# Gate of experts 2 to 6 in seven block products: 21 matmuls of 256 columns for 12 of 512, and the sums they need

## The reference, cut to what matters

```python
h = _layernorm(x) * (1 + cb) + sb
gate = einsum('btd,edf->ebtf', h, Wg)     # + low rank h @ Ga @ Gb for two of the experts
up   = einsum('btd,edf->ebtf', h, Wu)     # + low rank
mid  = silu(gate) * up
out  = einsum('ebtf,efd->ebtd', mid, Wd)  # + low rank
x    = x + gb * einsum('bte,ebtd->btd', router_weights(h), out)
```

## Time and profile before

| what | value |
|---|---|
| median of 3 runs | 804.85 us (803.84 to 805.88) |
| the profiled execution's own time | 805.75 us |
| its span, first to last instruction | 804.0 us |
| PE busy | 793.1 us, 99% of the span |
| POOL busy | 403.3 us, 50% |
| DVE, ACT busy | 508.3 us, 465.8 us |
| mean granted TensorE clock | 0.998 of full speed |

### The profile page before, as it was taken

One profiled execution on the slowest core, in us unless ns is written; L12 is line 12 of the kernel. 1 busy time (PEld: TensorE's weight loads), 2 busy tenths in 40 slices (PEclk: granted clock), 3 DMA queues, 4 the chain that ended last, 5 costly groups with the idle time before them and its releaser, 6 DMA issues.

```text
span 804.0 us, 14773 instructions
## 1 busy us (share of the span) xinstructions
PE 793.1 (99%) x5116; PEld 710.0 (88%) x5116; DVE 508.3 (63%) x1074; ACT 465.8 (58%) x1259; POOL 403.3 (50%) x547
## 2 busy tenths in 40 slices
PE   9899999999999999999999999999999999999997
PEld 8688899999999999999999999898888888888887
DVE  5667676475466667457557757666785454554575
ACT  5777677677577767767667866652553232332322
POOL 3767587486567567567657656220311010110493
PEclk9999999999999999999999999999999999999999
DMA  9200010000000000000000000202410110100002
GB/s 334 104 28 1 2 61 1 1 8 2 0 8 2 1 4 5 1 2 8 1 1 8 1 1 2 79 1 53 118 40 2 40 40 1 40 0 1 1 1 106
DMA packets 8329, 22.32 MB, mean 28 GB/s; under 512 B 1592, under 2 KB 4280, under 8 KB 8128
## 3 DMA queue, kind: packets, MB, share of 16 engines
q1 hardware_dynamic: 7680, 21.29, 7.9%
q10 hardware_dynamic: 576, 0.08, 0.1%
HBM read 19.26 MB, written 2.11 MB: 27 GB/s over the span
## 4 chain that ended last, share of the span: by engine, by line
PE 94%; DVE 2%; ACT 1%; issue 1%; POOL 1%; DMA 1%; ACTq 0%; DVEq 0%; POOLq 0%
PE ps_o L671 14%; PE ps_proj L548 9%; PE ps_proj L550 9%; PE ps_proj L549 9%; PE ps_s L548 7%; PE ps_s L549 7%; PE ps_s L550 7%; PE ps_turn L600 4%; PE ps_y L548 4%; PE ps_y L549 4%; PE ps_y L550 4%; PE ps_turn L618 3%; PE ps_turn L548 2%; PE ps_turn L549 2%; PE ps_turn L550 2%; PE ps_o L550 2%
## 5 line engine op out<-in xcount | busy, mean ns | idle before, releaser
L671 PE MATMUL ps_o<-vaug,probs 128*128 128x129 f32 x1024 | 136.1, 276 | 1.7 <-POOL probs L1674 0.9
L671 PEld LDWEIGHTS ps_o<-vaug,probs 128*128 128x128 f32 x1024 | 130.0, 192 | 8.0 <-POOL probs L1674 1.4
L993 ACT ACTIVATE ps_s<-ps_s,knorm 128x512 f32<-128x512 f32 x128 | 79.3, 657 | 96.2 <-PE ps_s L550 96.1
L1287 DVE RECIPROCAL rden<-ps_o 128x2 f32<-128x2 f32 x128 | 21.8, 170 | 155.5 <-PE ps_o L671 155.3
L1680 POOL TENSOR_TENSOR we_lo<-raw_e,we_hi 128x512 fp32r<-128x512 f32 x22 | 28.4, 1318 | 161.3 <-ACT we_hi L1036 161.3
L1257 DVE TENSOR_TENSOR prod<-ps_proj,cs 128x1024 f32<-128x1024 f32 x76 | 92.5, 1218 | 11.0 <-ACT sq L936 11.0
L1625 POOL TENSOR_TENSOR root<-ssq,powers 128x4 f32<-128x4 f32 x76 | 77.8, 1024 | 27.4 <-ACT sq L936 27.4
L936 ACT ACTIVATE sq<-ps_proj 128x128 f32<-128x128 f32 x304 | 80.1, 279 | 18.9 <-PE ps_proj L550 16.0
L1641 POOL TENSOR_TENSOR prod<-prod 128x512 f32<-128x512 f32 x62 | 80.1, 1292 | 10.0 <-DVE prod L1257 10.0
L548 PE MATMUL ps_proj<-w_hi,h_hi 128*128 128x512 f32 x192 | 83.3, 434 | 0.4 <-DVE h_lo L1204 0.4
L1672 POOL TENSOR_SCALAR_AFFINE_SELECT probs<-probs 128x256 f32<-128x256 f32 x64 | 26.4, 412 | 106.7 <-ACT probs L1001 106.4
(11 more groups left out here) (220 smaller groups left out, 2191.2 us busy)
## 6 DMA issues: line engine op xcount, KB each, us to landing
raw_e<-in_we SPq DMA_DIRECT2D x8, 768.0 KB, 4.4
raw_p<-in_wqkv SPq DMA_DIRECT2D x6, 512.0 KB, 8.5
raw_e<-in_wo SPq DMA_DIRECT2D x4, 512.0 KB, 12.7
x_all<-in_x SPq DMA_DIRECT2D x1, 1536.0 KB, 7.3
out<-acc SPq DMA_DIRECT2D x3, 512.0 KB, 2.6
x_all<-in_wmod SPq DMA_DIRECT2D x1, 1024.0 KB, 10.4
gates_a<-gate_rows_dram SPq DMA_DIRECT2D x8, 128.0 KB, 2.9
gates_b<-gate_rows_dram SPq DMA_DIRECT2D x1, 1024.0 KB, 10.2
```

The lines of the kernel that those rows point to most:

```text
L671: mm = pe.matmul(ps_o[:, h * (D + 1):(h + 1) * (D + 1)], probs[:, s % 2, at:at + P], vaug[b % 2][:, k, i // 2, :], start=(h == 0 and k == ...
L993: act.activation(ps_s[:, t, :], ps_s[:, t, :], ACT.Tanh, scale=knorm[:, b % 2, t, i // 2:i // 2 + 1]).then_inc(tanh_done, 1)
```

## The change: what it does

**The product.** For the tiles of experts 2 to 6 (8 to 27, `SEVEN` to `EIGHT`) gate is a 2 x 2 block product of weights (256 x 256) and tokens (256 x 512), made in seven products of blocks in place of eight. Each is one `three` of 256 columns. Four of the seven (`seven_first`) go ahead of up, the other three (`seven_last`) between up and the products with Wd. ACT copies the four first results to `seven`, POOL makes three sums of them, DVE adds two to the late results.

**What the blocks need.** Sums of blocks of the tokens (`sums_t`, four POOL instructions of 128x256 for each n) and of the weights (`sums_s`, four of 128x128 for each expert), and the high and low parts of these (`round_t`, `rest_t`, `round_s`, `rest_s`). The tokens of batches 4 and 5 are written to DRAM and read back, since their place is taken by then.

**The places.** `low_rank` and `fold` pieces move a tile earlier, split_e(2, 0) and (2, 1) move ahead within tiles 6 and 7, router piece 5 moves from tile 7 to 6, and `part` has a buffer for each n.

```diff
-LATE_ROUTE = {2 * NEXT + 3: [0], 2 * NEXT + 4: [1, 2], 2 * NEXT + 5: [3, 4], 2 * NEXT + 6: [5, 6, 7], 2 * NEXT + 7: [8, 9, 10, 11, 12]}
+LATE_ROUTE = {2 * NEXT + 3: [0], 2 * NEXT + 4: [1, 2], 2 * NEXT + 5: [3, 4, 5], 2 * NEXT + 6: [6], 2 * NEXT + 7: [7, 8, 9, 10, 11, 12]}
-LOW_STEPS = {NEXT + 1: [0, 1], NEXT + 2: [2], NEXT + 4: [3], NEXT + 5: [4, 5]}
+LOW_STEPS = {NEXT + 1: [0], NEXT + 2: [1, 2], NEXT + 3: [3], NEXT + 4: [4, 5]}
@@ PE
+            def seven_first(m):
...
+                if m == FIRST_OF[e]:
+                    pe.wait_ge(we_split, 3 * e - 1)
+                    pe.wait_ge(s_split, e - NL + 1)
+                if m == FIRST_OF[NL] + n:
+                    pe.wait_ge(t_split, 2 * n + 2)
+                if q:
+                    pe.wait_ge(quarter_silu, 2 * q - 1)
+                else:
+                    pe.wait_ge(mid_done, 2 * SEVEN - 1)
+                product_of(ps_s[:, 0, 0:S], of["A11"], of["B11"], True)
+                product_of(ps_s[:, 0, S:], of["S2"], of["T2"], False).then_inc(seven_ready, 1)
+                if q:
+                    pe.wait_ge(quarters_added, q)
+                product_of(ps_s[:, 1, 0:S], of["S1"], of["T1"], True)
+                product_of(ps_s[:, 1, S:], of["S3"], of["T3"], False).then_inc(seven_ready, 1)
+            def seven_last(m):
...
+                pe.wait_ge(seven_copied, 2 * q + 1)
+                product_of(ps_s[:, 0, 0:S], of["A12"], of["B21"], False).then_inc(gu_ready, 1)
+                pe.wait_ge(seven_copied, 2 * q + 2)
+                product_of(ps_s[:, 1, 0:S], of["S4"], of["B22"], False)
+                product_of(ps_s[:, 1, S:], of["A22"], of["-T4"], False).then_inc(gu_ready, 1)
+            for m in range(SEVEN, EIGHT):
+                seven_first(m)
+                up_alone(m)
+                seven_last(m)
+                down(2 * m - 2)
+                down(2 * m - 1)
@@ ACT
+            def round_t(n):
+                act.wait_ge(t_made, 4 * n + 4)
...
+                elif n == 2:
+                    act.wait_ge(t_split, 4)
+                    act.wait_ge(router, 3 * STEPS)
...
+                if m == NEXT + 2:
+                    round_s(NL)
                 mid_head(2 * m + 1)
...
+                if m == NEXT + 3:
+                    split_e(NL, 2)
+                    round_t(2)
+            for m in range(SEVEN, EIGHT):
+                copy_seven(m)
+                for e, m3 in SEVEN_SPLIT.get(m, ()):
                     split_e(e, m3)
+                if m in SEVEN_ROUND:
+                    round_s(SEVEN_ROUND[m])
+                if m == SEVEN + 2:
+                    round_t(3)
+                silu_seven(m)
+                mid_head(2 * m)
+                mid_head(2 * m + 1)
@@ DVE
+            for m in range(SEVEN, EIGHT):
+                add_quarters(m)
+                for g in (2 * m, 2 * m + 1):
+                    product_seven(g)
+                for g in (2 * m, 2 * m + 1):
+                    mid_tail(g)
+                accumulate(2 * m - 2)
+                accumulate(2 * m - 1)
@@ POOL
+            inv_std2(B - 1)
+            low_rest(0)
+
+            pool.wait_ge(h2_split, B)
+            sums_t(2)
+            split_e(NL, 0)
+            sums_s(NL)
+            rest_s(NL)
+            low_rest(1)
+            rest_t(0)
+            split_e(NL, 1)
+            rest_t(1)
+            for m in range(SEVEN, EIGHT):
+                sums_seven(m)
+                if m == SEVEN:
+                    split_e(NL, 2)
+                    rest_t(2)
+                if m == SEVEN + 1:
+                    sums_t(3)
+                if m == SEVEN + 2:
+                    rest_t(3)
+                if m in SEVEN_SUMS:
+                    sums_s(SEVEN_SUMS[m])
+                for e, m3 in SEVEN_SPLIT.get(m, ()):
                     split_e(e, m3)
+                if m in SEVEN_ROUND:
+                    rest_s(SEVEN_ROUND[m])
```

More of the change, by code:

```diff
@@ L522, in _ @@
             sp.wait_ge(router, 2 * STEPS)
+            for kept in h2_kept:
+                sp.wait_ge(kept, 16)
             expert(1)
@@ L846, in _ @@
                 slot(s)
-            for m in range(NEXT, len(TILES)):
+            for m in range(NEXT, SEVEN):
                 up(2 * m)
@@ L858, in _ @@
                     low_rank(i)
+            for m in range(SEVEN, EIGHT):
[4 more added lines that the diff above has]
+                down(2 * m - 1)
+                for i in LOW_STEPS.get(m, ()):
+                    low_rank(i)
+            for m in range(EIGHT, len(TILES)):
+                up(2 * m)
+                up(2 * m + 1)
+                down(2 * m - 2)
+                down(2 * m - 1)
             down(2 * len(TILES) - 2)
@@ L1391, in accumulate @@
                     dve.wait_ge(base_done, 2 * n + half + 1)
[L1392 to L1394 removed]
+                if e == NE - 1 and n == 0 and half == 0:
+                    dve.wait_ge(low_ready, 3 * NL)
                 for t in range(2):
@@ L1585, in _ @@
                         route(LATE, piece)
+            for m in range(SEVEN, EIGHT):
[6 more added lines that the diff above has]
+                accumulate(2 * m - 1)
+                for i in LOW_STEPS.get(m, ()):
+                    fold(i)
+            for m in range(EIGHT, len(TILES)):
+                product(2 * m)
+                product(2 * m + 1)
+                mid_tail(2 * m)
+                mid_tail(2 * m + 1)
+                accumulate(2 * m - 2)
+                accumulate(2 * m - 1)
             accumulate(2 * len(TILES) - 2)
@@ L1727, in slot @@
                         split_e(e, m3)
+                if s in SLOT_SUMS:
+                    sums_t(SLOT_SUMS[s])
                 return units[1:]
@@ L1740, in _, with low_rest @@
                 pending = slot(s, pending)
-            inv_std2(B - 1)
-            for e in range(NL):
+            def low_rest(e):
                 pool.wait_ge(low_rounded, 2 * e + 2)
+                pool.wait_ge(ln2_rstd, B) if e == 0 else pool.wait_ge(s_split, 1)
                 pool.tensor_tensor(lowA_both[R:P, e], lowA[R:P, e], lowA_both[R:P, e], ALU.subtract).then_inc(low_split, 1)
```

204 lines of the change are left out of this document (186 added, 18 removed).

## The result

The changed kernel takes 808.88 us (median of 6 runs, 807.09 to 809.65) where the kernel before takes 804.84 (6 runs, 803.84 to 805.88): a ratio of 1.0044, 95% interval 1.0028 to 1.0059. By the medians it is 4.0 us slower, by the ratio 3.5 (1.0044 x 804.85 = 808.4); 810 was predicted. The profiled execution took 809.65 us, the slowest of the six, with a span of 807.9. It is compared with the span of 804.0 before: +3.9.

The account below looks back on a forecast made before the run. PE bounds the kernel (busy 99%, 94% of the chain). Tile 9's start +10.0, the other 19 tiles -5.1 and tile 11 +0.4 give +5.3 on 804.85: 810.1, said as 810; own range 806.5 to 813, 8 in 10 801 to 813.

Parts of the forecast that it names:

- tile 9's start: End of the entry through tile 8: tile 9 at 613.6 against 603.6, +10.0 us with tile 8's gain included.
- The gain in PE's work: Gate of tiles 8 to 27: 21 matmuls of 256 columns replace 12 of 512, saving 0.24 to 0.29 us a tile.
- Steady state: Later seven-product tiles: PE takes 8.1 us each, slack 1 us or more at each step, so additions cost nothing.
- The 0.4 us at tile 11 to 12: Tightest tile, 11: POOL's sums, two splits and rest_s take 8.5 us against PE's 8.1, costing 0.4 us.
- POOL's list and product(14): Entry to tile 8: POOL's preparations end at 600.0; DVE, held by POOL, finishes product(14) at 597.7 instead of 591.1.
- The first wait: Ahead of tile 8's first gate matmuls: PE 4.1 us late, waiting for DVE's product(14).
- accumulate(12): DVE behind router pieces 7 to 12, six steps held by POOL: done at 609.7 instead of 599.1.
- The second wait: Ahead of tile 8's products with Wd: PE waits some 6 us, released by an accumulate on DVE.
- The mechanism: Entry: a DVE instruction reading two SBUF operands waits for the running POOL instruction's end, one such per POOL instruction.
- Rival 1: Entry: DVE is hardly held up by POOL, only 1.4 us lost; 801.3 us, chance 0.18.
- Rival 2: Entry: product(14) and copy late, but pieces 7 to 12 mostly fall in POOL's gap; 804 us, chance 0.15.
- Rivals 3 and 4: Gate pace of 256 columns: 0.125 with late entry, 812.3 us; or 0.13, gain only 0.2 us; chance together 0.07.

Follow-up runs that it names:

- the two runs that fill that wait: Changed kernel with low-rank matmuls repeated to keep PE busy in both waits (807.41 us, ratio 1.0031) or only the second (807.49 us, 1.0028).
- the two runs in which product(14) came early enough: Changed kernel with router pieces 3 to 6 behind product 15's mid_lo (812.17 us), or with POOL's entry instructions cut to 256 columns (804.72 us).
- moved preparations and whole pieces: Changed kernel with its preparations, router Exp, round_s and first-results copy in other places, POOL's instructions uncut: 803.69 us, ratio 0.9978 to the kernel before.
- run with halves: Changed kernel with POOL's entry instructions cut into pieces of 256 columns, preparations not moved: 804.72 us, ratio 0.9997 to the kernel before.
- first try: Changed kernel with POOL's four t_lo subtractions of token groups 0 and 1 moved ahead of tile 5's end: 806.77 us, ratio 1.0012.
- second wait filled: Changed kernel with six repeats of a low-rank step on PE ahead of tile 8's Wd products only: 807.49 us, ratio 1.0028.
- POOL's row beside the kernel before: Kernel before, with ten more POOL subtractions of 128x512 behind its split of expert 2's first weights, results unread: 814.70 us, ratio 1.0112.
- pieces moved: Changed kernel with router pieces 3 to 6 put behind mid_lo of index 15, together with pieces 7 to 12: 812.17 us, ratio 1.0075.

## Why the prediction was right, step by step

- **Time and direction.** 810 was said, 808.88 measured; slower, as forecast. +5.3 us was the sum and +3.9 is the trace's. That tile 9's start fits to 0.4 us is owed in part to luck: two errors of the entry, 2.1 us too much and 1.6 too little, cancel (below).
- **The gain in PE's work.** 5.1 us over the last 19 tiles was too small: 5.7 measured. The pace of 256 columns was 0.118 where 0.1196 was taken. Tiles take 8.03 to 8.16 us where 8.1 was said.
- **Steady state.** No wait in any tile from 9 to 27. The 0.4 us at tile 11 to 12 did not come.
- **POOL's list and product(14).** Forecast: done at 597.7; the row says 596.93 + 0.69 = 597.6. POOL's list was to end at 600.0 and ended at 596.58 + 2.90 = 599.5. The first wait, forecast 4.1 us, was 3.4. The list began 0.7 us later than said, since PE was 0.4 us earlier and not 0.8 and ACT's first Copy was done at 582.5 and not 581.8, and it grew by 1.1 us and not by some 2. One sum of the prediction is off (588.6 + 3.0 is 591.6, not 591.4), and nothing hangs on it, since DVE's next step ends with POOL's instruction in any case.
- **accumulate(12).** This step was mis-sized. It was to be done at 609.7, behind six hindered steps; it was done at 607.6. In pieces 7 to 12 five steps were hindered (0.69, 0.44, 0.63, 0.96 and 1.00 us), since POOL was idle from 599.5 to 601.8 and its sums of 128x256 take 0.74 and not 0.83. The second wait was 3.0 us where 6 was said: accumulate(12) came 2.1 us earlier, and PE came to it at 604.8 and not at 603.3.
- **The missing term.** PE's clock after a wait stood in the sum at nothing. By the timeline it costs 1.6 us behind the second wait, by the traces of the two runs that fill that wait 1.4 us, by their ratios 1.0 to 1.3 us (1.0031 and 1.0028 for 1.0044, with intervals that overlap); the one behind the first is hidden by the second wait (the same two runs). By the trace together: 2.1 too much for accumulate(12), 1.6 too little for the clock. Tile 9 starts at 613.2 where 613.6 was said.
- **The mechanism.** That POOL's instructions hold DVE up is shown, not only argued: ten of them alone slow the kernel before by 9 us, and cutting them in half without taking any away gives back 3.8. Rival 1 (DVE hardly held, 801.3) is out; its time is what comes of the change once the row of POOL is moved and cut, 800.0. Rival 2 (half of it, 804) is out by the second wait. Rivals 3 and 4 are out by the pace of 0.118. What the prediction had as a wait for DVE alone, ahead of tile 8, has POOL's own list as a second bound: 1.58 and 2.51 us of it are left, released by POOL, in the two runs in which product(14) came early enough.
- **Still open.** Why runs with the moved preparations and whole pieces scatter over 9 us. Their mean granted clocks go with the time: 0.990 to 0.995 in the four runs over 806 us, 0.997 to 1.000 in the four under 801. So a lower clock goes with the longer runs, but which comes of which isn't shown. Nor is whether PE's waits differ from run to run, by which of DVE and POOL comes first at each step: only one execution of that kernel, of 804.23 us, has a trace.

## What to carry to other kernels

Work moved to POOL because POOL is idle isn't free: count the DVE instructions beside it that work on SBUF alone, small ones too (TENSOR_REDUCE and RECIPROCAL were free here), and price each at up to the length of the POOL instruction that runs. If POOL's row can't go where DVE has nothing urgent, cut its instructions into shorter ones; here two of 256 columns took 1.44 us for one of 512 with 1.29, and the cut returned the whole loss. Look also at what else waits for POOL's list, which the cut makes longer. And when PE has two waits in a row, only what moves the end of the last one moves the time, the clock behind the first included.

## What the runs showed of the hardware

- Which DVE instructions wait for POOL: TENSOR_TENSOR, SCALAR_TENSOR_TENSOR and TENSOR_SCALAR on SBUF did, down to 128x4 (1.09 us for what takes 0.17); TENSOR_REDUCE (0.19) and RECIPROCAL (0.18) never did in the entry of the changed kernel, though POOL was working, nor did product and accumulate, which read PSUM (0.69 us, and 0.88 for two).
- The granted clock fell behind waits of PE of 2.51 us (0.76 in the 2.1 us that follow and 0.50 in the next 2.0, run with halves), 2.95 (first try: 0.64, then 0.50), 2.97 and 3.40 (changed kernel), 3.39 (0.61, second wait filled), 4.74 (0.50, POOL's row beside the kernel before) and 6.13 (0.50, pieces moved). It stayed at 1.00 behind waits of 1.19, 1.43, 1.58 and 1.73 us, and behind one of 3.28 us in the run with moved preparations and whole pieces (1.00 in the 3 us after it). So a wait of 3 us may or may not be charged. The Trainium skill (TensorE: Matmul & The Clock Gate, section "What's actually happening") has two clock levels only, and warns that the point of the switch varies from run to run. The rows agree with the two levels, since no stretch read here lies under 0.50; no kernel here was traced twice, so for the second no run shows it.
